# A metaformer block on one core: the second FFN layer's bias added to the tokens by VectorE instead of by a matmul per tile, and GpSimd's sum of t and beta released by a chunk's first sum

## The reference

```
t = _to_tokens(x)                    # (B, 2304, 256)
x_n = _ln_t(t)
h = gelu(x_n @ W1[e] + b1[e])        # 256 -> 512, for each expert e
y = h @ W2[e] + b2[e]                # 512 -> 256
out = sum over the two experts of w_e * y_e
t = t + layer_norm(out + x_n) * gamma + beta
```

## Time and profile before

| | us |
|---|---|
| median of 3 runs | 1001.24 (999.81 to 1005.07) |
| span of the profiled execution | 999.0 |
| PE busy | 927.6 (93%) |
| VectorE busy | 732.0 (73%) |
| ScalarE busy | 543.3 (54%) |
| GpSimd busy | 147.5 (15%) |

### The profile page before, as it was taken

How to read it: one execution, slowest core, us unless ns; L and a number is a source line. 1 busy time by engine, 2 the same in 40 slices (tenths; PEclk the granted TensorE clock), 3 DMA queues, 4 the chain that set the end, 5 groups by cost and what they waited for, 6 DMA issues and landing times. The chain is left out here.

```text
span 999.0 us, 18982 instructions
## 1 busy us (share of the span) xinstructions
PE 927.6 (93%) x7395; PEld 708.7 (71%) x7395; DVE 732.0 (73%) x1817; ACT 543.3 (54%) x985; POOL 147.5 (15%) x165
## 2 busy tenths in 40 slices
PE   2887999999999999979999947999999999999997
PEld 2776666777677667646999934777777777777776
DVE  4797466368647844977579857778978897888877
ACT  4795334435344512223456438576867777686751
POOL 1110000000000010100213221111211121122112
PEclk9998999999999999989999868999999999999999
DMA  9813111004101105454458446354255335424211
GB/s 219 215 48 95 49 48 48 25 5 129 53 25 53 39 24 157 144 161 89 115 151 231 126 127 143 95 126 95 62 152 106 64 80 159 97 53 92 64 33 48
DMA packets 135112, 96.02 MB, mean 96 GB/s; under 512 B 63611, under 2 KB 129548, under 8 KB 134924
## 3 DMA queue, kind: packets, MB, share of 16 engines
q1 hardware_dynamic: 135022, 94.81, 37.1%
HBM read 55.95 MB, written 29.40 MB: 85 GB/s over the span
## 5 line engine op out<-in xcount | busy, mean ns | idle before, releaser
L1273 PE MATMUL pM<-V,U 128*128 128x368 f16 (+3 forms) x2016 | 323.4, 316 | 0.0
L1273 PEld LDWEIGHTS pM<-V,U 128*128 128x128 f16 x2016 | 195.7, 98 | 103.2 <-issue 2.3
L1963 DVE SCALAR_TENSOR_TENSOR gl<-gf,sc,gh 128x384 f16<-128x384 f32 x192 | 147.9, 807 | 51.6 <-ACT gh L1776 51.5
L1785 ACT ACTIVATE gf<-pH,b1c,sc 128x384 f32<-128x384 f32 x192 | 127.8, 669 | 89.2 <-issue 73.4
L2094 PE MATMUL pH<-xT,w1h 128*128 128x384 f16 x768 | 158.2, 329 | 6.9 <-DMA xT<-xs 4.5
L2110 PE MATMUL pY<-w2h,gl 128*128 128x256 f16 x576 | 157.0, 273 | 0.0
L2110 PE MATMUL pY<-w2l,gh 128*128 128x256 f16 x576 | 157.0, 273 | 0.0
L2110 PE MATMUL pY<-w2h,gh 128*128 128x256 f16 x576 | 157.0, 273 | 0.0
L745 ACT CAST V<-pV 128x384 f16<-128x384 f32 x96 | 45.7, 478 | 156.3 <-PE pV L1244 156.3
L901 DVE TENSOR_TENSOR V<-pV,V 128x384 f16<-128x384 f32 x96 | 52.0, 552 | 88.6 <-ACT V L745 88.3
L1776 ACT ACTIVATE gh<-gf,sc 128x384 f16<-128x384 f32 x192 | 115.4, 616 | 0.0
(11 more groups left out here) (259 smaller groups left out, 1335.7 us busy)
## 6 DMA issues: line engine op xcount, KB each, us to landing
xa<-in_xt SPq DMA_DIRECT2D x16, 576.0 KB, 6.6
xs_scratch<-xs SPq DMA_DIRECT2D x16, 576.0 KB, 3.9
tk<-t_scratch SPq DMA_DIRECT2D x24, 384.0 KB, 3.9
out<-o SPq DMA_DIRECT2D x23, 384.0 KB, 2.9
xs<-in_ew SPq DMA_DIRECT2D x16, 512.0 KB, 4.2
U<-xs_scratch SPq DMA_DIRECT2D x16, 480.0 KB, 4.8
w1r<-in_ew SPq DMA_DIRECT2D x8, 512.0 KB, 4.3
w2r<-in_ew SPq DMA_DIRECT2D x8, 512.0 KB, 5.3
```

Source lines behind the costliest of these rows:

```text
L1273: return nc.tensor.matmul(out[:, :, first:end], U[:, k, hi_u, piece, :], V[:, b % 2, hi_v, k, c, :, first + TILES * d:end + TILES * d], st ...
L1785: nc.scalar.activation(gf[:, (JB * m + j) % GBUFS, :], pH[:, (JB * m + j) % HBUFS, 0:CN], ACT.Gelu, bias=b1c[:, j // FB, j % FB:j % FB + 1 ...
L1963: stt(gl[:, sl, j, :], gf[:, (JB * m + j) % GBUFS, :], scale_of(G_UP), gh[:, sl, j, :], ALU.mult, ALU.subtract).then_inc(g_step, 1)
```

## The change

The bias of the second layer no longer goes through PE. `split_b2`, `b2z`, `b2ones`, the scale B2_UP and the 72 matmuls of L2108 are gone; so are the two units of second-layer biases in the convolution part, with their DMAs and reductions. In their place VectorE adds the summed bias `b2c[:, 1]` to a chunk's normalised tokens `tnk` in SBUF, in place, one `tensor_tensor` of 128 x 768 float32 per chunk (`add_b2`), one chunk ahead of its `sum_up`; the first one stands ahead of the loop. `add_b2` comes after that chunk's `take_x`, so layer 1 still reads the tokens without the bias. On GpSimd, `add_beta(n)` now waits for the first sum of chunk n-1 instead of the end of `finish` of chunk n-2, and that of chunk 1 waits too.

```diff
...
 EXPERTS = 8
-B2_UNITS = 2
-UNITS_1, UNITS = EXPERTS + 1, 2 * EXPERTS + 1 + B2_UNITS
-STAGES, UNITS_SLOT = 3, {2: 2, 3: 3, 4: 3, 5: 3, 6: 4, 7: 2, 8: 2}
+UNITS_1, UNITS = EXPERTS + 1, 2 * EXPERTS + 1
+STAGES, UNITS_SLOT = 3, {2: 2, 3: 3, 4: 3, 5: 3, 6: 4, 7: 2}
 SUMS_AT = 448
...
             here = stage[u % STAGES]
-            if u in (EXPERTS, UNITS_1 + EXPERTS, UNITS_1 + EXPERTS + 1):
-                if u == EXPERTS:
-                    return eb1.rearrange("e p f -> p e f"), here[:, 0:EXPERTS * 4].rearrange("p (e f) -> p e f", e=EXPERTS)
-                part, h = EXPERTS // B2_UNITS, u - UNITS_1 - EXPERTS
-                return eb2.rearrange("(h e) c -> h (e c)", e=part)[h:h + 1].broadcast_to([P, part * C]), here[:, 0:part * C]
+            if u == EXPERTS:
+                return eb1.rearrange("e p f -> p e f"), here[:, 0:EXPERTS * 4].rearrange("p (e f) -> p e f", e=EXPERTS)
             e, w = (u, ew1) if u < EXPERTS else (u - UNITS_1, ew2)
...
 TOP = 2.0 ** 13
-V1, HB, V2, W1_UP, G_UP, W2_UP, W1_DOWN, Y_DOWN, B2_UP, NSC = range(10)
-SC_STEPS = 11
-B2_TOP = 2.0 ** 5
+V1, HB, V2, W1_UP, G_UP, W2_UP, W1_DOWN, Y_DOWN, NSC = range(9)
+SC_STEPS = 10
...
         tb = sb("tb", [P, 2, CT, C], F32)
-        b2z = sb("b2z", [P, C], F16)
-        b2ones = sb("b2ones", [P, P], F16)
         xs2 = sb("xs2", [P, 2, 2, CC, CT, P], F16)
...
         sc_step = sem("sc_step")
-        b2_step = sem("b2_step")
+        b2_added = sem("b2_added")
         y_ready = sem("y_ready3")
...
             nc.gpsimd.memset(mhalf[:, :], -0.5).then_inc(c_set, 1)
-            nc.gpsimd.memset(b2ones[:, :], 2.0 * B2_TOP / P).then_inc(c_set, 1)
-            pool.wait_ge(c_set, 3)
+            pool.wait_ge(c_set, 2)
...
                 pool.wait_ge(tk_loaded[m % TBUFS], 48 * (CHUNKS // TBUFS * b + m // TBUFS + 1))
-                if not (is_first(b) and m < 2):
-                    pool.wait_ge(z_step, (n - 1) * Z_ALL)
+                if not (is_first(b) and m == 0):
+                    pool.wait_ge(z_step, (n - 1) * Z_ALL + 1)
                 nc.gpsimd.tensor_tensor(tb[:, s], tk[:, m % TBUFS], bet[:, None, :].broadcast_to([P, CT, C]),
...
                 s.did(tt(scale_of(Y_DOWN), scale_of(V2), scale_of(HB), ALU.mult))
-                s.settle()
-                s.did(nc.vector.tensor_scalar(scale_of(B2_UP), scale_of(W2_UP), scale_of(G_UP), 1.0 / B2_TOP,
-                                              ALU.mult, ALU.mult))
                 s.at(SC_STEPS)
...
-            def split_b2(b):
-
-                s = Steps(dve, b2_step, b, 2)
+            def add_b2(b, m):
+
+                n = CHUNKS * b + m
                 dve.wait_ge(bias_step, 3 * (b + 1))
-                after(dve, y_ready, CT * CHUNKS * b)
-                s.did(nc.vector.tensor_scalar(b2z[:, :], b2c[:, 1, :], scale_of(B2_UP), None, ALU.mult))
-                s.settle()
-                low = slice(P // 2, P)
-                s.did(stt(b2z[low, :], b2c[low, 1, :], scale_of(B2_UP)[low], b2z[low, :], ALU.mult, ALU.subtract))
+                dve.wait_ge(xl_ready, n + 1)
+                tt(tnk[:, m % NBUFS], tnk[:, m % NBUFS], b2c[:, 1, None, :].broadcast_to([P, CT, C]),
+                   ALU.add).then_inc(b2_added, 1)
...
                 s.settle()
+                dve.wait_ge(b2_added, n + 1)
...
                 dve.wait_ge(z_step, n * Z_ALL)
+                dve.wait_ge(b2_added, n + 1)
                 dve.wait_ge(bias_added, n + 1)
...
             split_w2(0, high=True)
-            split_b2(0)
+            add_b2(0, 0)
...
                         split_w2(b)
-                        split_b2(b)
                     if later(b, m, 1, CHUNKS):
...
                         take_x(*later(b, m, XAHEAD, CHUNKS))
+                    if later(b, m, 1, CHUNKS):
+                        add_b2(*later(b, m, 1, CHUNKS))
                     if m == CHUNKS - 2 and later(b, m, 2, CHUNKS):
...
         def _(pe):
-            pe.wait_ge(c_set, 3)
+            pe.wait_ge(c_set, 2)
...
                     pe.wait_ge(w2_step, 2 * (b + 1))
-                    pe.wait_ge(b2_step, 2 * (b + 1))
                 for t in range(CT):
...
                     terms = [(j, g, w) for j in range(JB) for g, w in ((gh, w2h), (gh, w2l), (gl, w2h))]
-                    nc.tensor.matmul(pY[:, t, 0:C], b2ones[:, :], b2z[:, :], start=True, stop=False)
                     for i, (j, g, w) in enumerate(terms):
...
                                                 w[:, j // FB, j % FB, :],
-                                                start=False, stop=(i == len(terms) - 1))
+                                                start=(i == 0), stop=(i == len(terms) - 1))
                     last.then_inc(y_ready, 1)
...
             pe.wait_ge(r_step, R_STEPS)
```

## The result

| | before | after |
|---|---|---|
| median of 5 runs each, us | 1004.62 (999.81 to 1005.64) | 993.52 (993.09 to 995.79) |
| ratio of the times, 95% interval | | 0.992 [0.9896, 0.9943] |
| span of the profiled execution | 999.0 | 993.1 (a run of 995.79) |

A second comparison (seven runs of the changed kernel beside 30 of the one before) gave 995.3 against 1000.95, a ratio of 0.9934 [0.9909, 0.996]. So the change gains 0.7 to 0.8% by these ratios; 992.8 was forecast, and faster.

The account below looks back on a forecast made before the run. PE, busy 95.91 of 95.91 us in an image's FFN windows, was taken as the bound. -7.5 - 1.15 - 0.15 + 0.4 = -8.4 us, off the median 1001.24, gave 992.8 us; range 989.0 to 996.5.

Parts of the forecast that it names:

- The matmuls: FFN's second layer: 69 of 72 bias matmuls leave PE's chain at 0.109 us each, the last chunk's don't count; -7.5 us.
- The start: FFN's first second layer: PE waits for the weights' low part instead of `b2z`, and low parts end earlier; -1.15 us.
- The constant: Before the FFN's first matmul: the memset of `b2ones` leaves the chain; -0.15 us.
- The adds: VectorE, one in-place add per chunk, taken as 956 ns: hidden inside its waits in ordinary chunks; 0 us.
- GpSimd's sum: `tb` now runs beside the sums `z` and the statistics, over before `rstd` is due; 0 us.
- An image's first chunk: The add stands before the first gelu's `sum_b2`, delaying PE's layer 1 by 0.13 us, three times; +0.4 us.
- The units: Convolution part: two reductions and two DMAs go, but PE's large wait comes from an earlier unit; 0 us.
- rival 1: The convolution part shifts without the two units: gain to 990.5 or loss to 995.8 us; chance 0.08.
- rival 3: VectorE becomes the bound, needing 101.0 us per image: 19 us slower, 1020 us; chance 0.03.
- rival 2: PE stalls at each image's first chunk, 3.3 us more than forecast: 996.1 us; chance 0.04.

Follow-up runs that it names:

- changed_gelu_early: Changed kernel with an image's first gelu waiting only for the copy of the first layer's biases: 993.87 us, ratio 0.9928 to the kernel before.
- before_beta_moved: Kernel before with only GpSimd's sum `tb` released by the first sum of the chunk before: 1000.42 us, ratio 0.9989 to the kernel before.
- before_no_units: Kernel before without the two units of second-layer biases in the convolution part: 1001.48 us, ratio 1.0001 to the kernel before.
- changed_beta_old: Changed kernel with GpSimd's sum released as in the kernel before: 994.29 us, ratio 0.9912 to the kernel before.
- changed_again: The changed kernel itself, run and profiled once more with no edit: 995.3 us, ratio 0.9934 to the kernel before.
- changed_matmul_back: Changed kernel with one matmul of zeros per tile put back on PE, adds kept: 1002.92 us, ratio 1.0002 to the kernel before.
- changed_units_spread: Changed kernel with the convolution part's remaining units spread over one more slot, two by two: 987.05 us, ratio 0.9847 to the kernel before.

## Why the prediction was right or wrong, and the step that failed

**The matmuls** (-7.5): right. In changed_gelu_early, without the first chunks' cost, the body is 360.52 - 353.09 = 7.43 us shorter for 68 matmuls, 0.109 each, and the 69th is the 0.11 by which the start's end moves. The tail is 14.56 against 14.61, so the last chunk's three didn't count, as said.

**The start** (-1.15): this is the step that failed, at the sentence that PE had done layer 1 by 622.35 and was not in the way. PE's pace in that sentence was one execution's, the margin between it and the weights was 0.05 us, and a wait of 2.36 us stood just ahead. In the changed kernel PE came out of the same wait at 1.2 GHz, and was 1.1 us later than the weights. Of the 1.15 nothing came: 35.72 is 35.80 less 0.11 for the matmul and 0.03 more. The saving on VectorE's side was sized right: with PE kept at work it is 1.24 - 0.11 = 1.13 us. The adds and the missing matmuls are not what slows PE: before_beta_moved, which has neither, shows the same four matmuls in 1.46 us. Ten profiled executions have this wait unfilled. In eight the four matmuls took 1.46 us, in two, the kernel before and before_no_units, 0.82. Those two have GpSimd's sum at its old place, but changed_beta_old has it there too, and took 1.46. So its place alone doesn't decide it, and why the two kept the clock stays open.

**The constant** (-0.15): PE's first wait in the FFN went from 1.91 to 1.77 us, released by `mhalf`. Right.

**The adds** (0): 0.951 us against 0.956 taken from the PSUM row. PE doesn't wait for them in an ordinary chunk. The sums begin a little later, as worked out: those that waited for PE did so 17 times for 14.2 us in the kernel before, and 5 times for 4.0 us in the changed one. VectorE's timeline in one, to lay beside the earlier trace rows:

```profile
658.29 2.20 DVE L1950 SCALAR_TENSOR_TENSOR gl<-gf,sc,gh 128x384 f16<-128x384 f32 x4
661.46 1.03 DVE L1869 SCALAR_TENSOR_TENSOR xs<-tnk,xs 128x384 f16<-128x384 f32 x2 [0.97 <-ACT xs L1760]
662.41 0.95 DVE L1932 TENSOR_TENSOR tnk<-tnk,b2c 128x768 f32<-128x768 f32 x1
663.27 0.87 DVE L1962 SCALAR_TENSOR_TENSOR z<-pY,sc,tnk 128x256 f32<-128x256 f32 x2
...
667.73 0.62 DVE L1950 SCALAR_TENSOR_TENSOR gl<-gf,sc,gh 128x384 f16<-128x384 f32 x1 [1.32 <-ACT gh L1768]
```

Four low parts take 2.20 instead of 3.76 us. Of that 1.56, `take_x` can use only a part, since it now waits 0.97 for ScalarE, as worked out; the add stands in the rest, and the wait of 1.33 us behind is 1.32.

**GpSimd's sum** (0): its place held, and it took 1.81 us instead of the 2.06 that I allowed. Its timeline:

```profile
663.90 1.80 POOL L1710 TENSOR_TENSOR tb<-tk,bet 128x768 f32<-128x768 f32 x1 [12.23 <-DVE z L1962]
...
666.48 0.86 POOL L1716 TENSOR_TENSOR rstd<-ve,mhalf 128x3 f32<-128x3 f32 x1 [0.78 <-DVE ve L1978]
```

It starts behind the first `z` and ends 0.78 us ahead of `rstd`. "0" is right for the sum of both edits, but the two were not priced one against the other: alone it is 0, and with the adds it is worth 1.5 us, since it makes the room for them at an image's start. Here the Trainium skill's page "SBUF — State Buffer", section "Who interferes with whom", says that a VectorE instruction with two SBUF inputs contends with a GpSimd instruction that reads SBUF, and one with at most one SBUF input doesn't. The trace agrees: `gl` 2175 ns beside `tb` and 617 without, `z` under 486 ns and `tb` 1.81 us beside each other.

**An image's first chunk** (+0.4): +0.26, the term's mechanism shown by changed_gelu_early. The layer pieces grew by 0.09 us each, where I took 0.13.

**The units** (0): right, by before_no_units. PE's wait was 5.51 and is 5.74 us, but it was 5.46 in before_no_units and 5.62 in before_beta_moved, which has all units, so 0.2 us there is scatter. The sign that I had named for rival 1, a convolution part that ends more than 1 us off 587, was seen (589.5), but it was no sign of that: 1.24 us of it stood ahead of 415 us in one execution, and 415.18 in changed_again. **VectorE as the bound** (rival 3): in the image from 711.60 to 805.82 us it is busy for 76.03 of 94.22 us in the changed kernel and 84.05 in changed_beta_old, against the 101 that the rival needed. **PE stalls at first chunks** (rival 2, +3.3): it is the right place and the right order. It takes a second add (2.6 us), or GpSimd's sum at its old place (1.5), to get there.

Of 8.4 us forecast, 7.17 + 0.08 + 0.13 (the constant, in convolutions III) = 7.4 came in the stages that the change touches. The start is short by 1.2, and the first chunks gave 0.1 back. In the spans 990.6 was forecast and 993.1 came: the start, and 1.4 us of scatter in the convolutions. That the medians, 992.8 and 993.52, lie within 0.7 us is partly luck: a second set of runs of the same kernel gave 995.3, and the median of before went from the 1001.24 that I started from to 1004.62 and back to 1000.95.

## What to carry to other kernels

An instruction of a saturated engine is priced by the step in the chain, not by its duration (0.109, not 0.273 us); measured as 0.109 on 68 of them. Where two engines arrive at a join within some tenths of a us of each other, removing one's work buys only what the other leaves, and that other engine's pace has to be read with what it did just before, its clock included. An added operation is hidden where the engine waits anyway, so look for the one stage that has no such wait (here an image's first chunk) and ask there whether all parts of the edit are needed together.

## What the runs showed of the hardware

**One wait, two clocks.** Behind a wait of 2.35 or 2.36 us at the FFN's start, PE ran at 2.4 GHz in two executions and at 1.2 GHz in eight, in the changed kernel until 3.1 us behind the wait; with the wait filled with matmuls it stayed at 2.4. Layer 1's last 30 matmuls then took 6.41 us, where at full clock they take 30/48 of 7.80, 4.88. Of these 1.5 us, 1.1 showed, since the weights' low part would have been waited for anyway.

**The scatter of the run times.** Convolutions III took 109.0 to 109.7 us in eight executions, 112.8 to 113.3 in four and 111.2 in one. Windows of PE and its clock, the kernel before first, then changed_matmul_back (the columns are those of the earlier trace rows):

```profile
486.00:494.00 8.00, 8.00 (x78) 8.00 (x76) 6.42 (x28) 4.01 (x9) 1.83 (x4) 1.00 0.86 232
494.00:502.00 8.00, 8.00 (x79) 8.00 (x78) 3.64 (x15) 3.50 (x6) 1.37 (x2) 1.00 0.59 157
```

```profile
486.00:494.00 8.00, 8.00 (x65) 8.00 (x64) 6.42 (x28) 3.27 (x7) 2.12 (x4) 0.82 0.89 232
494.00:502.00 8.00, 8.00 (x60) 7.82 (x58) 3.27 (x15) 2.49 (x5) 0.43 (x1) 0.76 0.21 47
```

PE is busy all the time in both, but the granted clock falls in the second, at 491 us, within a group of matmuls with a moving side of one column (1.00 in 489.4 to 491, 0.52 in 491 to 493):

```profile
489.45 2.91 PE L1392 MATMUL pA<-U,xs 120*128 120x1 f32 x20
```

The same twenty took 2.36 us in the kernel before. The other three long executions show 2.94 to 2.97 for them and the same fall, and convolutions III is 3.2 to 3.6 us longer in the four. In the one of 111.2 (changed_units_spread) the group took 2.36 and the clock fell a little behind it, for a shorter time. The two groups of run times of before, near 1000 and near 1005, lie somewhat further apart than that. None of the four kernels' edits touches that stretch; what decides it wasn't tried. That the fall causes the upper group is inferred from the sizes, since each trace is of one execution.
